# Attention output stage: the vector engine's and the sync engine's slots in another order

## The reference

```python
sim1 = jnp.einsum('bhid,bhjd->bhij', q, k_l)
attn1 = jax.nn.softmax(sim1, axis=-1)
out = attn1 @ attn2_inv @ (attn3 @ v)
out = out + res                  # res: 33 tap convolution of v along the tokens
out = out.transpose(0, 2, 1, 3).reshape(b, n, h * dh)
out = out @ w_out + b_out
t = t + (x + out)                # attention reads x = _ln_t(t)
...
Wx = jnp.einsum('bti,hi->bth', _ln_t(t), W)   # and its mean and variance over all tokens
```

## Time and profile before

| what | value |
|---|---|
| median of 3 runs | 5994.0 us |
| the profiled execution's own time | 5990.76 us |
| its span in the profile | 5989.0 us |
| output phase: first `scores` to last | 2591 to 3642 us |
| busy in the whole span | PE 88%, ACT 54%, DVE 50%, POOL 28% |

### The profile page before, as it was taken

The page is one execution under the profiler, slowest core; times in us unless marked ns, Lnnn a source line. Parts: engine busy times, 40 slices in busy tenths (PEclk is TensorE's granted clock), DMA queues, the critical chain, the costliest instruction groups (busy, mean ns, idle before and its releaser), DMA issues. The chain is left out here.

```text
span 5989.0 us, 209173 instructions
## 1 busy us (share of the span) xinstructions
PE 5279.7 (88%) x90148; PEld 3235.7 (54%) x90240; DVE 2984.9 (50%) x7660; ACT 3250.9 (54%) x9351; POOL 1679.4 (28%) x2016
## 2 busy tenths in 40 slices
PE   5599999997788987789999997888888888888888
PEld 4499888896566666644444443333333333333333
DVE  8577777775788885568888885000000000000000
ACT  5455555564677775379999994333333333333333
POOL 2100000002888884347777874000000000000000
PEclk7799999999999999999999999999999999999999
DMA  8722111125878783357888873111111111111111
GB/s 356 280 101 85 57 57 57 65 81 187 248 242 241 233 245 94 102 153 228 229 231 229 230 217 110 45 45 49 47 45 49 47 47 48 45 49 47 45 49 31
DMA packets 857847, 755.65 MB, mean 126 GB/s; under 512 B 71024, under 2 KB 732528, under 8 KB 853872
## 3 DMA queue, kind: packets, MB, share of 16 engines
q1 hardware_dynamic: 841840, 642.91, 36.0%
q0 software_dynamic: 13664, 99.32, 4.1%
q10 hardware_dynamic: 1440, 0.33, 0.0%
HBM read 425.72 MB, written 308.45 MB: 123 GB/s over the span
## 5 line engine op out<-in xcount | busy, mean ns | idle before, releaser
L2608 ACT ACTIVATE f_y<-f_acc 128x16 f32<-128x16 f32 x4096 | 749.8, 183 | 1547.8 <-PE f_acc L2574 1547.8
L2574 PEld LDWEIGHTS f_acc<-f_y,f_vT 128*32 128x32 f32 x32768 | 645.8, 108 | 1490.8 <-ACT f_y L2608 1490.8
L2574 PE MATMUL f_acc<-f_y,f_vT 128*32 128x16 f32 x32768 | 1045.6, 193 | 296.7 <-ACT f_y L2608 0.4
L2563 PE MATMUL f_junk<-f_idle 128*32 128x512 bf16 x12368 | 1225.4, 376 | 0.1
L2519 DVE TENSOR_TENSOR f_sum<-f_turned,f_t 128x512 f32<-128x512 f32 x128 | 88.5, 691 | 2071.6 <-PE f_turned L2556 2071.5
L2273 DVE TENSOR_REDUCE o_m<-o_bank_l 128x8 bf16<-128x512 f32 x512 | 327.2, 680 | 103.6 <-PE o_bank_l L2039 103.4
L2563 PEld LDWEIGHTS f_junk<-f_idle 128*32 128x32 bf16 x12368 | 368.6, 99 | 0.4 <-issue 0.4
L470 POOL DMA_DIRECT2D hidden<-l_h x46 | 34.6, 754 | 1166.9 <-DVE l_hsum L730 961.5
L1184 ACT ACTIVATE a_p<-a_s 128x512 f32<-128x512 f32 x512 | 264.0, 603 | 178.3 <-PE a_s L1068 178.2
L653 ACT ACTIVATE l_gate<-l_pf,l_bf 128x256 f32<-128x256 f32 (+7 forms) x512 | 202.1, 446 | 230.0 <-PE l_pf L580 229.9
L2224 ACT ACTIVATE o_p<-o_bank_s 128x512 f32<-128x512 f32 x512 | 264.3, 603 | 34.1 <-PE o_bank_s L2062 33.2
(11 more groups left out here) (284 smaller groups left out, 11564.2 us busy)
## 6 DMA issues: line engine op xcount, KB each, us to landing
o_v<-vals SPq DMA_DIRECT2D x256, 272.0 KB, 3.5
a_hid<-hidden SPq DMA_DIRECT2D x112, 520.0 KB, 5.1
skew<-gn_skew POOLq DMA_DIRECT2D x8, 6144.0 KB, 23.7
hidden<-l_h POOLq DMA_DIRECT2D x46, 1040.0 KB, 6.8
l_x<-skew SPq DMA_DIRECT2D x46, 1024.0 KB, 5.2
vals<-a_v SPq DMA_DIRECT2D x128, 272.0 KB, 3.3
gn_x<-in_x SPq DMA_DIRECT2D x16, 2048.0 KB, 16.7
a_xin<-in_x SPq DMA_DIRECT2D x128, 256.0 KB, 4.9
```

What stands on the lines that cost most here:

```text
L2563: nc.tensor.matmul(junk[rows, :], idle[:, 0:QUAD], idle[:, :], start=True, stop=True)
L2574: mm = nc.tensor.matmul(acc[k % 2][rows, t, :], vT[:, rows], before, start=False, stop=True, skip_group_check=True)
L2608: nc.scalar.activation(y[q][:, u, :], acc[u // RC % 2][:, u % RC, :], ACT.Sigmoid).then_inc(s_y, 1)
```

## The change

Two queues get another order; no instruction is added or taken away.

On DVE, `reciprocals(k-1)` goes ahead of `residual(k-3)`. The second half of `residual` (drain and four `bn_aggr`) becomes a function `moments`, which is called behind `normalise(k-2)` and ahead of `add_convolved(k-2)`. In the last slots, written out one by one, `moments` follows `residual` at once, as before.

On SP a slot becomes `spread(k-1)`, `pack(k)`, `store_wx(k-5)`, `store_t2(k-3)`, `load_base(k+1)`, `broadcast(k-1)`, two `load_v`, `load_tokens`.

```diff
@@ def slot(b, c, q, first, last) of SP
+                if precedes(c, 1, first):
+                    spread(b, c - 1)
+                pack(b, c)
                 if precedes(c, 5, first):
                     store_wx(b, c - 5)
                 if precedes(c, 3, first):
@@ -1893,7 +1896,7 @@
                     if follows(c, 1, last):
                         load_base(*at(b, c + 1))
                 if precedes(c, 1, first):
-                    spread(b, c - 1)
+                    broadcast(b, c - 1)
 
                 if c < GT and b + 1 < B:
                     wait(sp, "conv", NG * (b + 1))
@@ -1901,9 +1904,6 @@
                 if c >= GT and b + 2 < B:
                     wait(sp, "conv", NG * (b + 1) + GT)
                     load_v(b + 2, 0, c - GT)
-                if precedes(c, 1, first):
-                    broadcast(b, c - 1)
-                pack(b, c)
@@ def residual of DVE
                 for k in range(GT):
                     nc.vector.bn_stats(st[:, k, :], out[:, k, :])
+
+            def moments():
                 dve.drain()
@@ def slot(b, c, q, first, last) of DVE
+                if precedes(c, 1, first):
+                    reciprocals(b, c - 1)
                 if precedes(c, 3, first):
                     residual(b, c - 3)
-                if precedes(c, 1, first):
-                    reciprocals(b, c - 1)
                 if precedes(c, 2, first):
                     normalise(b, c - 2)
+                if precedes(c, 3, first):
+                    moments()
+                if precedes(c, 2, first):
                     add_convolved(b, c - 2)
```

## The result

The kernel after takes 6195.56 us (median of 4 runs, 6193.76 to 6203.38), the kernel before 5992.47 beside it: a ratio of 1.034 with a 95% interval of 1.0328 to 1.0352. The sign was forecast, the size was not: +203 us instead of +16, far outside the range. The profiled span is 6192.0 us.

The account below looks back on a forecast made before the run. PE's own instructions were taken to bound an undisturbed slot. The terms summed to 5990.8 - 18 + 5 + 17 + 7 + 5 = 6006.8 us, so a median of about 6009 (+0.25%), range 5979 to 6034.

Parts of the forecast that it names:

- 23 denominator waits: DVE's reciprocals wait for packed denominators in 23 slots; moving them first removes these, winning 18 of 20 us.
- the terms for late transfers: On SP's queue: v loads 17 us, base load 7 us, spread waiting for the previous broadcast 5 us.
- the scratch: SP's spread waits for the previous broadcast's landing: a third of slots, 0.3 each, 5 us; bounds 0 and 18 us.
- ACT's copies are ready by then: On SP, pack follows the spread from 6.6 us into the slot, with ACT's copies ready by that time.
- The base term: Base load issued 2.6 us later, 0.5 late for ACT's first scaling: 86 slots, 7 us; bounds 0 and 21 us.
- The term for v: Every fourth slot's second v load lands 0.59 us late for PE's convolution: 17 us; bounds nothing and 40 us.
- The estimate of 2.6 us for a v load: Landing time from 2.0 us fixed cost plus bytes at 436 GB/s; v and base not late, sum some 29 us lower.
- DVE: Moments behind the product make merge wait for POOL's subtraction: 4 to 5 us taken; bounds 0 and 24 us.
- Rival 3: DVE turns into the bound, merge colliding with POOL's subtraction in every slot: 6028 to 6045 us; chance 0.13.
- the margin of 0.04: DVE's next maxima end at 3.36 against PE's need at 3.40, so an ordinary slot loses nothing.
- Undisturbed slots stay at 8.15: Sign that the forecast is right: slots without waits keep their 8.15 us.
- Rival 4: Spread still waits, now for the scratch, so pack is no earlier and v is late too: 6016 us; chance 0.04.

Follow-up runs that it names:

- both rings open: The changed kernel with two scratches used in turn and the packs moved behind the base load: 6024.75 us, 1.005 of the kernel before.
- the order with four spreads: Kernel before with a 16-row scratch, four spreads, and SP's stores, base and v loads ahead of spreads, pack and broadcast: 6124.71 us, 1.0211.

## Why the prediction was right about the sign and wrong about the size

*Right.* PE, not DVE, bounded an undisturbed slot, and 0.33% was about all there was to win: with the slow broadcast replaced, in a kernel that leaves out the denominators, 0.4% (0.26 to 0.54) is won and a slot takes 8.17. The 23 denominator waits went. Line 2084 waits for v at all 29 places, ACT's line 2194 for the base, SP's line 1877 for the broadcast, though in every slot and not in a third of them. POOL's small sum takes 0.20. The merge takes 1.33 and ends at 3209.73, 0.55 behind the subtraction's end at 3209.18; 0.54 was taken. The issue times held: spread to broadcast at least 4.11 us, where 9.45 - 5.44 = 4.0 was worked out. The sign is right in part by luck: the terms for late transfers come to 29 us, where over 200 were needed, and the largest causes of the loss are not among them.

*The step that failed: the scratch.* It was priced at 5 us, at most 18, as a chance lateness: "a third of the slots to wait, 0.3 each". Two things were wrong.

- The broadcast's own latency was never read; "other transfers of this size" gave 3.5 to 3.9. In the trace of before it is 4.21 on average. With the new distance the ring is 4.1 + 4.2 = 8.3 us in a slot of 8.15: closed before anything else changes. A wait in such a ring is not paid once, it is the length of each slot. That comparison, the sum of the steps once around against the slot, was missing.
- Latencies of the old order were carried into the new one. Behind base, broadcast, two v loads and tokens without a gap the broadcast takes 5.26, so the ring has 4.4 + 5.3. The prediction itself says that from the spread on the queue runs without a gap, but took nothing for it, and even a shorter base latency. The base did land sooner, in 3.3 us; the broadcast and v did not.

*The step that was missing: packs ahead of the base load.* "ACT's copies are ready by then" was true for a base in time. The copies stand behind `scale_base` in ACT's queue, and the base load now behind the packs in SP's. The base term, 7 us, was therefore no term but the entry to a ring. Moving the packs behind the base load gives back 103 to 136 us, the largest single piece, though part of that comes through the broadcast and v, which then land sooner. The part on moved steps named what the packs' move does to the packs, not what it does to the base that feeds ACT ahead of them.

*v.* The mechanism was right and the size off: 17 us taken, the bound of 4.9 us every time gave 40, 92.7 measured. With both rings open it is 34.1 us, with a v load at 4.4 in the median where 4.1 was taken. The term for v was thus half of what it should have been even by itself, since v now stands right behind the broadcast. The sum has no term for the clock, which is half behind waits of this length, for 116 us of the phase. The estimate of 2.6 us for a v load was far off too, 5.2 being the median here; the Trainium skill gives the fit behind it (DMA: Bandwidth & Descriptors, Anatomy of one DMA) for DMAs issued from GpSimd, and these are issued from SP.

*DVE.* 5 us were taken, bounds 0 to 24; the moved moments alone cost 15 (8 to 21 by the interval). Rival 3 was right that the margin of 0.04 isn't there, and was not what made the loss: in the kernel after PE waits only 6.8 us for the maxima. "Undisturbed slots stay at 8.15" holds only for slots that the rings leave alone. Rival 4 was nearest in kind, a spread that waits for the scratch, and was dropped with the comparison of 0.8 against 2 us, which is no sum around the ring.

What stays open: how much of a landing time behind the broadcast is due to its 8 DMA engines, to repeated reads of the same rows, or to the number of transfers in flight. The Trainium skill says that each DMA engine consumes the descriptors of its queue in order (DMA: Bandwidth & Descriptors, Queues, rings and completion order), which fits packs that land with the broadcast ahead of them, at 4.85 us; but 16 rows in the old order moved the packs' landing only from 3.09 to 2.74. How the 203 us divide among the two rings, the v waits and the slower clock also stays open, since each edit moved several of them.

## What to carry to other kernels

When a queue is put in another order, write down each ring that goes through it (issue, landing, the consumer, what stands behind the consumer on its engine, the next issue), add it up once around with the transfer's own latency, and compare with the slot; a ring as long as the slot is the new bound, and a wait in it is paid every slot. Don't carry a DMA's latency from an order with gaps into one without: read it for the transfer by what stood ahead of it. And first ask what makes the late transfer late, here a broadcast directly ahead of it, before moving everything that waits.

## What the runs showed of the hardware

- The same pair of small packs lands in 1.78 us right behind the spread, 2.42 behind the base load, 3.09 behind broadcast in the kernel before, and 4.85 behind v loads and broadcast.
- A load's issue on SP is not a fixed cost: a base load takes 0.64 us on average before and 0.94 where tokens, v loads and stores are issued right ahead of it. Two v loads take 1.0 us in the kernels before and after, and 1.7 on average in the order with four spreads.
- PE's granted clock was half in 29 stretches of the kernel after, each behind a gap of PE of 1.9 to 4.6 us, and PE was busy for 107 of their 116 us; in the kernel before, where the longest gap of this phase is 1.0 us, it stayed full.
- A broadcast that reads 8 rows leaves 8 landing events and takes 4.2 us on average, where a plain load of the same bytes takes 3.4 in its place; the packs behind it land in 3.1 and 2.3. 16 rows shorten the broadcast to 4.02 in the same order.
